# A four-phase fp32 block on one core: paired weight columns in two small projections, another order of work in attention and in block 6 of the FFN

## What is computed

```python
gate_logits = jnp.einsum('bsd,ed->bse', x, gate_w)          # 8 experts
zxbcdt = x @ in_proj_w.T
dt = jax.nn.softplus(zxbcdt[..., -NHEADS:] + dt_bias)        # 4 heads
```

## Time and profile before

| | |
|---|---|
| median of 3 runs | 557.07 us (556.97 to 557.43) |
| the profiled execution | 557.08 us |
| its span, first to last instruction | 555.3 us |
| granted TensorE clock, mean | 0.996 |
| PE busy | 523.4 us, 94% |
| DVE busy | 402.6 us, 73% |
| ACT busy | 310.6 us, 56% |
| POOL busy | 126.9 us, 23% |

### The profile page before, as it was taken

The page is one execution under the profiler, slowest core; times in us unless marked ns, Lnnn a source line. Parts: engine busy times, 40 slices in busy tenths (PEclk is TensorE's granted clock), DMA queues, the critical chain, the costliest instruction groups (busy, mean ns, idle before and its releaser), DMA issues. The chain is left out here.

```text
span 555.3 us, 9124 instructions
## 1 busy us (share of the span) xinstructions
PE 523.4 (94%) x3049; PEld 441.6 (80%) x3049; DVE 402.6 (73%) x897; ACT 310.6 (56%) x768; POOL 126.9 (23%) x272
## 2 busy tenths in 40 slices
PE   5998899999999979999989999999998999999996
PEld 4777799999998967688878888757777778878885
DVE  5534465665665878799787899866886677878767
ACT  3655877688687643474343455988662254333332
POOL 2332434344243310000000003569433000000000
PEclk9999999999999999999999999999999999999999
DMA  7320000000002103000030000000000000000101
GB/s 267 112 78 1 18 22 2 1 1 2 2 2 102 47 1 138 1 1 1 5 129 0 2 0 1 1 1 2 1 0 2 0 1 1 1 1 0 39 1 38
DMA packets 5790, 14.25 MB, mean 26 GB/s; under 512 B 624, under 2 KB 2928, under 8 KB 5744
## 3 DMA queue, kind: packets, MB, share of 16 engines
q1 hardware_dynamic: 5744, 13.66, 6.9%
HBM read 12.61 MB, written 1.05 MB: 25 GB/s over the span
## 5 line engine op out<-in xcount | busy, mean ns | idle before, releaser
L167 PE MATMUL psum<-xT_hl,ffn_w_hl 128*128 128x512 f32 x312 | 77.8, 397 | 3.1 <-DVE f_t L1232 3.1
L167 PE MATMUL psum<-f_um,ffn_w_hl 128*128 128x512 f32 x288 | 72.6, 399 | 1.4 <-DVE f_t L1232 1.3
L167 PEld LDWEIGHTS psum<-xT_hl,ffn_w_hl 128*128 128x128 f32 x312 | 56.3, 188 | 15.0 <-issue 4.0
L167 PEld LDWEIGHTS psum<-f_um,ffn_w_hl 128*128 128x128 f32 x288 | 53.2, 188 | 14.8 <-DVE f_um L1244 3.1
L1129 ACT ACTIVATE f_sil<-psum 128x512 f32<-128x512 f32 (+1 forms) x48 | 28.6, 596 | 63.1 <-PE psum L167 62.8
L1232 DVE TENSOR_TENSOR f_t<-psum,f_sil 128x512 f32<-128x512 f32 (+1 forms) x48 | 33.2, 691 | 30.0 <-ACT f_sil L1129 29.3
L691 DVE TENSOR_TENSOR pT_hl<-psum,pT_hl 126x360 fp32r<-126x360 f32 (+1 forms) x44 | 23.6, 537 | 42.9 <-ACT pT_hl L598 42.9
L167 PE MATMUL psum<-wo_hl,oT_hl 128*128 128x256 f32 x384 | 50.8, 282 | 4.0 <-DVE oT_hl L697 4.0
L167 PE MATMUL psum<-xT_hl,wq_hl 128*128 128x512 f32 x192 | 52.3, 407 | 1.9 <-ACT qT L566 1.9
L167 PEld LDWEIGHTS psum<-wo_hl,oT_hl 128*128 128x128 f32 x384 | 47.7, 188 | 7.5 <-DVE oT_hl L697 5.9
L566 ACT ACTIVATE qT<-psum 128x512 f32<-128x512 f32 x32 | 34.9, 1091 | 31.6 <-PE psum L167 31.6
(11 more groups left out here) (238 smaller groups left out, 1130.4 us busy)
## 6 DMA issues: line engine op xcount, KB each, us to landing
w_raw<-in_wq SPq DMA_DIRECT2D x4, 512.0 KB, 4.1
w_raw<-in_wo SPq DMA_DIRECT2D x4, 512.0 KB, 3.2
ffn_w_raw<-in_ffn SPq DMA_DIRECT2D x3, 576.0 KB, 5.7
ffn_w_raw_far<-in_ffn SPq DMA_DIRECT2D x3, 576.0 KB, 5.0
ssd_w_raw<-in_ssd SPq DMA_DIRECT2D x3, 512.0 KB, 5.0
x_resid<-in_x SPq DMA_DIRECT2D x2, 512.0 KB, 4.4
out_x<-x_resid SPq DMA_DIRECT2D x4, 256.0 KB, 2.2
w_raw<-in_wk SPq DMA_DIRECT2D x1, 512.0 KB, 6.3
```

What stands on the lines that cost most here:

```text
L167: i = e.matmul(dst, lhs(a), rhs(b), start=start and n == 0, stop=stop and n == len(TERMS) - 1, **kw)
```

## The change

1. **Paired columns.** For the router the high and the low weights now stand side by side as 16 columns of one stationary operand, and each k block takes two matmuls (with the high and the low part of x) instead of three. The same for dt, whose weights the host now packs twice (4 + 4 columns); DVE overwrites the second 4 high columns with the low ones (one small copy, `dtw`, behind the subtraction `w_lo0`). The product low x low is now included. The two halves come out as 16 (8) rows; DVE adds them with a tensor_reduce in place of a copy in `top`, and with an added tensor_reduce ahead of the bias for dt.
2. **Attention, first loop.** ACT's `exps` of the first units come behind the copy of `v_hl` of the same j, and those of unit 0 are cut in two pairs (j = 5 and 6); the reciprocals come one j later. The eighth chunk of queries (`Q_PAIR` = 7) goes to bank 7 and does not wait for the copy of the seventh.
3. **Attention, DVE.** `oT_lo` comes ahead of `add`, and `norm0` at step 45 ahead of it too.
4. **FFN block 6.** PE issues `base_lora(6)` ahead of `second(5)`; DVE writes masked operands 2 and 3 in step 5 and all of 4 to 7 at the head of step 6.
5. Six and three one-count semaphores of the router's softmax become two that count (`top_dve`, `top_pe`); what is waited for stays the same.

```diff
@@ attention: tables @@
-            RECIPS = {NJ - 5: 0, NJ - 3: 1}
+            RECIPS = {NJ - 4: 0, NJ - 2: 1}
+            EXPS = {NJ - 6: (0, (0, 1)), NJ - 5: (0, (2, 3)), NJ - 4: (1, range(NB_Q)), NJ - 2: (2, range(NB_Q))}
+            Q_PAIR = 2 * GROUP - 1
@@ queries (pe) @@
-                    if n:
+                    if n and n != Q_PAIR:
                         e.wait_ge(s_qt, n)
                     for k in range(KB):
-                        m = three(e, bank(6), lambda w: wq_hl[:, g % 2, w, k, h * HD:(h + 1) * HD],
+                        m = three(e, bank(7 if n == Q_PAIR else 6), lambda w: wq_hl[:, g % 2, w, k, h * HD:(h + 1) * HD],
@@ project (pe) @@
                     e.wait_ge(s_wl, WO[g])
+                    e.wait_ge(s_qt, Q_PAIR + 1)
@@ first loop (act) @@
                 for j in range(NJ):
-                    if j in FIRST_UNITS:
-                        exps(FIRST_UNITS[j])
                     e.wait_ge(s_v, j + 1)
                     e.activation(v_hl[0:NK[j], HI, j, :], bank(4 + j % 2)[0:NK[j], :], ACT.Copy).then_inc(s_vhi, 1)
                     if j < GROUP:
                         q_evac(j)
+                    if j in EXPS:
+                        exps(*EXPS[j])
@@ main loop (dve) @@
                         pT_lo(i - LAG_P)
+                    if 0 <= i - LAG_F < NU:
+                        oT_lo(i - LAG_F)
+                    if i == NU + 1:
+                        early(phase, "norm0", e)
                     if i in y_tile:
                         add(y_tile[i])
                         if y_tile[i] >= (KV - 1) * NT:
                             early(phase, "stats", e, y_tile[i] % NT)
-                    if 0 <= i - LAG_F < NU:
-                        oT_lo(i - LAG_F)
-                    for step, stage in ((NU, "veps0"), (NU + 1, "norm0"), (NU + 2, "lo0"), (NU + 3, "logits_copy0"),
-                                        (NU + 4, "split0")):
+                    for step, stage in ((NU, "veps0"), (NU + 2, "lo0"), (NU + 3, "logits_copy0"), (NU + 4, "split0")):
@@ logits @@
                 for k in range(KB):
-                    m = three(e, bank((1, 6)[h]),
-                              lambda w: gw_hl[:, (w * KB + k) * EXPERTS:(w * KB + k) * EXPERTS + P],
-                              lambda w: xT[:, w, k, half(h)], k == 0, k == KB - 1)
+                    for w in (HI, LO):
+                        m = e.matmul(bank((1, 6)[h]), gw_hl[:, k * GW_K:k * GW_K + P], xT[:, w, k, half(h)],
+                                     start=k == 0 and w == HI, stop=k == KB - 1 and w == LO)
@@ top (dve) @@
-                e.tensor_copy(lg[:, seg], bank((1, 6)[h])[:, 0:32]).then_inc(FS["lgc"], 1)
+                e.tensor_reduce(lg[:, seg].rearrange("p (t n) -> p t n", t=HT),
+                                bank((1, 6)[h])[:, 0:HT * GW_K].rearrange("p (t w n) -> p t n w", t=HT, w=2),
+                                AX.X, ALU.add).then_inc(FS["lgc"], 1)
@@ ffn (pe) @@
-                        if i == MASK_STEP + 2:
-                            second(i - 1)
                         base_lora(e, i)
...
-                    if 2 <= i <= N and i != MASK_STEP + 2:
+                    if 2 <= i <= N:
                         second(i - 1)
@@ ffn (dve) @@
                         masked(1, 0, 1)
+                    if i == MASK_STEP + 2:
+                        masked(1, 4, 5, 6, 7)
                     if i < N and i != 1:
                         slot(i, 0)
                     if i == MASK_STEP + 1:
-                        masked(1, 2)
-                    if i == MASK_STEP + 2:
-                        masked(1, 4, 5)
+                        masked(1, 2, 3)
...
-                        masked(1, 3)
                         mask_diff(1)
-                    if i == MASK_STEP + 2:
-                        masked(1, 6, 7)
@@ mixer: w_lo0 (dve), in_proj (pe), dt (dve) @@
+                e.wait_ge(S["wl"], W_ORDER.index("0") + 1)
+                second = lambda w: w0[w][:, KB * P:2 * KB * P].rearrange("p (k n) -> p k n", k=KB)[:, :, NH:DT_ROWS]
+                e.tensor_copy(second(HI), f32(second(LO))).then_inc(S["dtw"], 1)
...
+                if b == 1:
+                    e.wait_ge(S["dtw"], 1)
+                    for k in range(KB):
+                        for w in (HI, LO):
+                            m = e.matmul(bank(IN_BANK[n]), w_part(b, HI, k), xT[:, w, k, half(h)],
+                                         start=k == 0 and w == HI, stop=k == KB - 1 and w == LO)
...
-                e.tensor_tensor(t3(V), t3(bank(7)[:, 0:NT * NH]), repeat(par[:, PR_DTB:PR_DTB + NH], NT),
-                                ALU.add).then_inc(S["dt_dve"], 1)
+                e.tensor_reduce(t3(V), bank(7)[:, 0:NT * DT_ROWS].rearrange("p (t w h) -> p t h w", t=NT, w=2),
+                                AX.X, ALU.add).then_inc(S["dtv"], 1)
+                e.wait_ge(S["dtv"], 1)
+                e.tensor_tensor(t3(V), t3(V), repeat(par[:, PR_DTB:PR_DTB + NH], NT), ALU.add).then_inc(S["dt_dve"], 1)
```

More of the change, by code:

```diff
@@ L565, in q_evac, with exps @@
                         e.wait_ge(s_s, g * NJ)
-                    e.activation(qT[:, HALF * half:HALF * half + HALF, h], bank(6), ACT.Copy,
+                    e.activation(qT[:, HALF * half:HALF * half + HALF, h], bank(7 if n == Q_PAIR else 6), ACT.Copy,
                                  scale=float(HD) ** -0.5).then_inc(s_qt, 1)
-                def exps(u):
+                def exps(u, some=None):
                     e.wait_ge(s_max, u + 1)
@@ L573, in exps @@
                     rows, parts, p = probs(u)
-                    for n in range(parts):
+                    for n in range(parts) if some is None else some:
                         m = e.activation(p[:, n, :], p[:, n, :], ACT.Exp, bias=NEGM[0:rows, u % 4, n:n + 1],
                                          accum_out=DEN[0:rows, u % 4, n:n + 1])
-                    m.then_inc(s_exp, 1)
+                    if n == parts - 1:
+                        m.then_inc(s_exp, 1)
                 w_hi(e, 3)
@@ L802, in build @@
         FS = {n: sem(f"ffn_{n}") for n in F_EVENTS}
+        TOP_DVE = {n: i + 1 for i, n in enumerate(("mt", "gm", "dg", "nmc", "rs", "wt"))}
+        TOP_PE = {n: i + 1 for i, n in enumerate(("mtT", "nm", "sum"))}
         def ffn(tag, first, before):
@@ L1016, in pe @@
                 base_x(e, 1, (1,))
-                need(e, "mt", 1)
-                e.transpose(bank(7)[0:2, 0:P], MT, ident).then_inc(FS["mtT"], 1)
+                need(e, "top_dve", TOP_DVE["mt"])
+                e.transpose(bank(7)[0:2, 0:P], MT, ident).then_inc(FS["top_pe"], 1)
                 lora_a(e, 1, (0,))
-                need(e, "dg", 1)
-                e.matmul(bank(7)[:, P:P + 2], ones[0:2, :], DG, start=True, stop=True).then_inc(FS["nm"], 1)
+                need(e, "top_dve", TOP_DVE["dg"])
+                e.matmul(bank(7)[:, P:P + 2], ones[0:2, :], DG, start=True, stop=True).then_inc(FS["top_pe"], 1)
                 lora_a(e, 1, (1,))
                 need(e, "ex", SLOTS)
-                e.matmul(bank(7)[:, P + 2:P + 4], ones, SUM, start=True, stop=True).then_inc(FS["sum"], 1)
+                e.matmul(bank(7)[:, P + 2:P + 4], ones, SUM, start=True, stop=True).then_inc(FS["top_pe"], 1)
                 base_lora(e, 0)
@@ L1559, in in_proj @@
                     bank_taken(e, former[-1])
-                for k in range(KB):
-                    m = three(e, bank(IN_BANK[n]), lambda w: w_part(b, w, k), lambda w: xT[:, w, k, half(h)],
-                              k == 0, k == KB - 1)
+                if b == 1:
[4 more added lines that the diff above has]
+                                         start=k == 0 and w == HI, stop=k == KB - 1 and w == LO)
+                else:
+                    for k in range(KB):
+                        m = three(e, bank(IN_BANK[n]), lambda w: w_part(b, w, k), lambda w: xT[:, w, k, half(h)],
+                                  k == 0, k == KB - 1)
                 m.then_inc(S["ip"], 1)
@@ L1724, in dt_copy @@
                     e.wait_ge(S["ip"], n + 1)
-                    e.activation(dt_in[0:NH, half(h)], bank(IN_BANK[n])[0:NH, :], ACT.Copy).then_inc(S["ipz"], 1)
+                    e.activation(dt_in[0:DT_ROWS, half(h)], bank(IN_BANK[n])[0:DT_ROWS, :], ACT.Copy).then_inc(S["ipz"], 1)
                 def silu_z(n):
```

59 lines of the change are left out of this document (32 added, 27 removed).

## The result

The changed kernel takes 543.49 us (median of 4, 543.28 to 543.99); the kernel before, beside it, 557.02 us (median of 4). The ratio is 0.9758, 95% interval 0.9741 to 0.9775: 13.5 us faster, where 545.6 was forecast. The profiled execution took 543.31 us, its span is 541.5 against 555.3.

What follows compares the result with a forecast made beforehand. PE's own work (busy 94% of the span) and its waits were taken to bound the kernel; 3.0 + 1.0 + 2.7 + 1.3 - 0.2 + 3.7 = 11.5 off 557.1 gave 545.6 us, own range 544.3 to 547, outer range 543.4 to 549.4.

Steps and rivals of the forecast that it cites:

- the one at 99.17: Middle of attention, two projections in succession: PE's wait for `oT_lo` and `add` stays and becomes one for x_resid.
- Start of attention: Attention's first loop: two waits for `v_hl` go (1.5 us) and the query pair gains 1.4 to 1.5; 3.0 us together.
- Middle: Middle of attention: `p_v` no longer waits for `oT_lo` behind `add`, 0.33 us once in each of three groups; 1.0 us.
- End and into the FFN: Attention's last steps: projections, norm and transposes come earlier, the last projection by 3.5 us; 2.7 us is left.
- The split: End of attention: DVE's 1.95 us split of the first FFN weights now holds back the last `add`, leaving 2.7 of 3.5.
- Router and dt: Router and mixer's dt: twelve matmuls fewer, 2.8 us of PE's work, of which 1.3 comes through; the small copy costs 0.2.
- Block 6: Block 6 of both FFNs: PE's wait for `gated(5,1)` goes (1.5 us), operands 6 and 7 are ready (0.33); 1.85 each.
- PE busy down by 2.8: Sign in the profile after: PE's busy time over the whole kernel falls by about 2.8 us.
- a rival at another place: Rival: new waits near 196 and 204 us make the clock fall there too, costing about 1.5 us; 547.1, chance 0.08.
- a chance of 0.05 to vanish: More than forecast: the half-clock stretch at 428 us vanishes as well, 1.5 us less; 544.1, chance 0.05.
- DVE keeps its end: Rival: DVE and ACT pace attention's last ten steps; end and middle terms shrink from 3.7 to 1; 548.3, chance 0.15.
- the slower one: Rival: `add` behind `oT_lo` delays each of 32 projections by up to 0.52 us; some 9 us slower, 566, chance 0.02.

Runs made afterwards that it cites:

- a_pool_split: The changed kernel with the split of the first FFN's first weights done by POOL instead of DVE; median 544.80 us.
- b_order: The kernel before with only DVE's order in attention changed (`oT_lo` and `norm0` ahead of `add`); median 554.63 us, ratio 0.9948.

## Why the prediction was right, and where it was off

- **The total was right with some luck.** 543.49 lies 0.1 us inside the outer range. The terms were 0.3 off together; 0.44 at the start and 1.53 from the absent stretch came on top. With the stretch the kernel would have taken about 545.0, near the 545.6.
- **What bounds the kernel** held: PE's own work and its waits. Of the waits named in the prediction, those for `v_hl`, for the query copy (1.26), for `xn` and for `gated(5,1)` went, the one at 99.17 changed its name, and at the end of attention two for `oT_hl` are left: 1.14 at 192.75, longer than the 0.67 it had, and the new one of 0.93. The 1.27 ahead of the last projection shrank to 0.26, for `x_resid`.
- **Start of attention, 3.0, measured 3.45.** The mechanism held (tile 7 at 43.28 by the old head, forecast 43.4; pair 2.85 us for twelve matmuls). The size was off because I summed the idle times in brackets, 1.27 and 0.26. By distances between starts, the measure that I had announced myself, the two waits are 2.01 - 0.56 = 1.45 and 0.99 - 0.55 = 0.44: 1.9, not 1.5. The bracket leaves out what the modelled end of the last matmul covers.
- **Middle, 1.0, measured 0.70.** The three gains of 0.33 came. What failed is "there the wait only changes its name": where two projections follow each other, PE now waits 0.42 for `add` instead of 0.34 for `oT_lo`, and each group gives back about 0.1.
- **End and into the FFN, 2.7, measured 2.65.** Step by step against the forecast, net of what came before: projection 0.44 (0.5), next 1.44 (1.5), transposes 2.54 (2.9), next projection 1.55 (1.9) with a new wait of 0.93 (1.1), last 3.02 (3.5). The split did keep the last `add` back. a_pool_split shows its price: 0.65.
- **Router and dt, 1.1 with the copy, measured 1.2.** The second FFN gave 0.47 and 0.43, where I had 1.0 with a bit for the half clock; the first dt 0.34 instead of 0.1, the second 0.16 instead of 0.2 to 0.3, the copy -0.2 as said. The added tensor_reduce took 0.22 us, forecast 0.2. Four router matmuls take 0.93 us (428.68 to 429.61), 0.233 each.
- The Trainium skill (TensorE: Matmul & The Clock Gate, section Back-to-back issue gap) would have given 0.7 for this term by its 131 ns a matmul. The trace does not agree: two matmuls less are 0.47 us, and the term without the small copy is 1.4 (1.2 with it).
- **Block 6, 1.85 each, measured 1.92 and 1.98.** Right in size, and `gated(4,1)` was no trouble. The forecast named two causes, the silu behind `second(5)` and the masked operands, and did not say what each is worth. They overlap: the first alone gives 1.0, the second alone 1.54, both 1.92.
- **PE busy down by 2.8**: 6.4, as told above.
- **What was missing** are the clock and the start. I had the stretch as a rival at another place (1.5 slower) and as a chance of 0.05 to vanish (1.5 faster), as if the trace of before showed what every execution does. It shows one execution of a kernel that has the stretch in two of three. The right treatment was a term of its own, the price 1.5 by a rate that the change can move either way, and another half a microsecond or so of spread at the start. Both rivals about `add` (DVE keeps its end; the slower one) fell: the `x_resid` waits come to 1.5 us in 4 places, not in 32.

What stays open: why this pause and not a longer one brings the stretch (in the trace of the kernel before PE also pauses 1.36 us at 281.63 and 1.37 at 398.00, with the clock at 1.00 behind both), why the rate follows the distance in the way it does, what it is between 406.4 and 410.0, and why the same kernel's rate differs between rounds. Rates from 4 to 6 executions are rough (the changed kernel's own is 0 of 4), and the pause was filled in one kernel only, with its parent in another round.

## What to carry to other kernels

Price a wait on PE by the distance between starts, before and beside it, not by the idle time that a row prints; and where a wait has two causes, run each half alone, since their gains need not add up (1.0 and 1.54 gave 1.92). A gain of 1 us can vanish behind a clock stretch that comes in some executions only, at a rate that an edit far away can change: look at the mean clock of each execution before you believe or drop such a gain, and fill the pause ahead of the stretch with idle matmuls.

## What the runs showed of the hardware

- A pause of PE of 1.03 us at the mixer's end is followed, 1.3 to 2.1 us after its end, by 3.3 to 3.5 us at half the clock, but only in some executions of the same kernel: 41 of 62 of the kernel before. It costs 1.5 us in the traces. With delays of 1 to 2 us elsewhere the rate was 9 of 12 after 0 of 6, and 1 of 6 after 4 of 5.
- The Trainium skill (TensorE: Matmul & The Clock Gate, section The HAM clock gate) says that the throttled state is the default and that activity releases it. The runs agree as far as they go: in the profiled executions the half clock came back within the kernel's work only behind PE's pause of 1.03 us, in 4 of 13, and it was in none of 5 executions where that pause was filled.
- The same twelve idle matmuls and what follows them to the first key matmul take 3.1 to 4.4 us at the start of an execution. They start every 0.43 us at first and every 0.22 us later, with a granted clock shown as 1.00 throughout, and the rate doubles at a different moment in each trace (b_order near 13.1 us, the changed kernel near 10.3). Executions without the stretch still differ by up to 1.9 us (554.9 to 556.9 for the kernel before).
- A tensor_reduce from PSUM, 64 values of each partition to 32, takes 0.22 us; the copy of 32 that it replaced took 0.18.
